# Attention, first group: who copies the last block's features, and how denominators are inverted

## The reference, cut to what matters

```python
H, d_head, scale = 16, 16, 6.0 ** -0.5
L_q = exterior(q1, q2)            # (B, T, H, 6), each of unit length
JL_k = exterior(k1, k2) @ J6.T
attn = einsum('bqhc,bkhc->bhqk', L_q, JL_k) * scale
attn = softmax(where(causal, attn, -inf), axis=-1)
v = (x @ W_v + b_v).reshape(B, T, H, d_head)
out = einsum('bhqk,bkhd->bqhd', attn, v).reshape(B, T, D)
return out @ W_o + b_o
```

## Time and profile before

| | us |
|---|---|
| median of 3 runs | 1147.47 |
| lowest, highest | 1146.25, 1149.84 |
| the profiled execution | 1146.05 |
| its span | 1144.3 |
| TensorE busy (matmuls) | 1036.2 |
| ScalarE busy | 874.3 |
| VectorE busy | 737.8 |
| GpSimd busy | 457.7 |

### The profile page before, as it was taken

The page is one execution under the profiler, slowest core; times in us unless marked ns, Lnnn a source line. Parts: engine busy times, 40 slices in busy tenths (PEclk is TensorE's granted clock), DMA queues, the critical chain, the costliest instruction groups (busy, mean ns, idle before and its releaser), DMA issues.

```text
span 1144.3 us, 23937 instructions
## 1 busy us (share of the span) xinstructions
PE 1036.2 (91%) x7549; PEld 564.4 (49%) x7549; DVE 737.8 (64%) x1471; ACT 874.3 (76%) x1251; POOL 457.7 (40%) x671
## 2 busy tenths in 40 slices
PE   8998999989888788998899898989899999999996
PEld 4457999946555121222122222222223578999844
DVE  6898788768997524434254657467758686445656
ACT  4226777746787999999999999999997237787710
POOL 1003666457730423422221322431312445677755
PEclk8999999999899899999999999999999999999999
DMA  8911555445776221020201122020100955566654
GB/s 288 276 57 49 172 164 170 154 129 168 211 220 193 66 71 51 11 66 10 65 11 31 40 70 80 26 78 19 48 1 19 300 171 157 162 189 184 185 163 153
DMA packets 125718, 133.82 MB, mean 117 GB/s; under 512 B 13224, under 2 KB 111888, under 8 KB 125616
## 3 DMA queue, kind: packets, MB, share of 16 engines
q1 hardware_dynamic: 109056, 90.95, 25.1%
q0 software_dynamic: 14448, 39.47, 12.4%
q10 hardware_dynamic: 2112, 2.10, 0.5%
HBM read 80.43 MB, written 52.04 MB: 116 GB/s over the span
## 4 chain that ended last, share of the span: by engine, by line
PE 30%; ACT 25%; issue 14%; DVE 8%; DVEq 1%; SPq 0%; POOL 0%; DMA 0%; ACTq 0%; POOLq 0%
ACT wide L2073 23%; PE banks L2445 6%; PE banks L1957 5%; PE banks L2370 4%; PE banks L2459 3%; PE banks L2379 2%; PE banks L1931 2%; PE banks L2433 1%; PE banks L1453 1%; PE banks L1456 1%; DVE x_res L1628 1%; DVE wide L1677 1%; PE banks L1971 1%; DVE attn_lines_parts L190 1%; PE banks L1455 1%
## 5 line engine op out<-in xcount | busy, mean ns | idle before, releaser
L2073 ACT ACTIVATE wide<-banks 128x1536 f32<-128x1536 f32 (+1 forms) x384 | 492.3, 1491 | 4.2 <-PE banks L1931 3.1
L1957 PE MATMUL banks<-wide,attn_attend_v_now 128*32 128x512 f32 (+3 forms) x2560 | 288.7, 542 | 2.4 <-POOL wide L2083 2.3
L2083 POOL TENSOR_SCALAR_AFFINE_SELECT wide<-wide 128x256 f32<-128x256 f32 (+1 forms) x320 | 115.9, 391 | 389.9 <-ACT wide L2073 387.4
L1931 PE MATMUL banks<-attn_attend_q_now,attn_attend_k_now 32*128 32x512 f16 (+3 forms) x1280 | 150.9, 355 | 56.8 <-ACT wide L2073 53.7
L1931 PEld LDWEIGHTS banks<-attn_attend_q_now,attn_attend_k_now 32*128 32x128 f16 x1280 | 38.7, 91 | 292.4 <-ACT wide L2073 248.5
L668 POOL DMA_INDIRECT f_region<-xn_rows,f_token_of x79 | 78.7, 996 | 125.1 <-DVE f_token_of L899 82.6
L2128 DVE COPY sums<-banks 128x512 f32<-128x512 f32 x32 | 22.1, 691 | 134.5 <-PE banks L1957 134.2
L2133 DVE RECIPROCAL below<-below 128x512 f32<-128x512 f32 x32 | 107.3, 3353 | 1.1
L2445 PE MATMUL banks<-f_xnt 128*128 128x128 f32 x752 | 100.3, 276 | 4.3 <-DVE f_more L2671 2.7
L2558 POOL DMA_INDIRECT last_rows_in<-xn_rows,f_spare x72 | 69.1, 960 | 64.0 <-DVE f_stage L2619 23.7
L2445 PEld LDWEIGHTS banks<-f_xnt 128*128 128x128 f32 x752 | 91.3, 191 | 6.6 <-issue 4.8
(11 more groups left out here) (368 smaller groups left out, 1783.3 us busy)
## 6 DMA issues: line engine op xcount, KB each, us to landing
y_half<-f_xnt SPq DMA_DIRECT2D x94, 128.0 KB
y_slots<-wide SPq DMA_DIRECT2D x79, 128.0 KB
attn_v<-f_more SPq DMA_DIRECT2D x32, 256.0 KB, 3.6
attn_attend_v_now<-attn_v SPq DMA_DIRECT2D x32, 256.0 KB, 3.2
x_res<-L_attn_x SPq DMA_DIRECT2D x8, 512.0 KB, 7.6
xn_rows<-f_w_all SPq DMA_DIRECT2D x8, 512.0 KB, 4.6
attn_q<-attn_lines_q_out SPq DMA_DIRECT2D x8, 512.0 KB, 3.4
attn_k<-attn_lines_k_out SPq DMA_DIRECT2D x8, 512.0 KB, 4.1
```

The costliest lines, as they stand in the source:

```text
L1931: last = pe.matmul(score[i % SLOTS][:, j, column:column + columns(u)], k_now[rows, kt * P:(kt + 1) * P], q_now[rows, qc * QW + c0:(qc + 1) ...
L1957: last = pe.matmul(out_bank[qc][rows, c0:QW], v_now[:, kt, rows], probs[:, place, column:column + columns(u)], start=(kt == 0), stop=(u == ...
L2073: act.activation(probs_flat[:, at:at + width_of[i]], score_flat[i % SLOTS][:, 0:width_of[i]], ACT.Exp, scale=SCALE).then_inc(sem.exp_done, 1)
L2083: pool.affine_select(out=part, in_=part, compare_op=ALU.is_ge, fill=0.0, base=0, pattern=[[0, part.shape[1]], [1, P]], channel_multiplier= ...
```

## The change

VectorE makes the second copies of the last block, right before its first chunk, and keeps the four turned parts behind its second chunk, one after the other; ScalarE does neither any more. TensorE's and SyncE's lists stay. The denominators are turned in 32x32 blocks, so that each block has them in one column; the 16 columns are inverted and turned back with each column repeated 32 times. The multiplication is the same.

```diff
-    def copy_last(act):
-        second_copies(act, BLOCKS - 1, (BLOCKS - 1) % 2)
-
-    def keep_last(act, part, held):
+    def copy_last(dve):
+        q = (BLOCKS - 1) % 2
+        dve.wait_ge(sem.parts_ready, BLOCKS)
+        both = feats[:, q, 0, :, 0:4 * PL].rearrange("p n (a c) -> p n a c", a=2)
+        dve.tensor_copy(both[:, :, :, PL:], both[:, :, :, 0:PL])
+        dve.tensor_copy(feats[:, q, 1, :, 2 * PL:4 * PL], feats[:, q, 1, :, 0:2 * PL]).then_inc(sem.feats_ready, 1)
+
+    def keep_last(dve, part, held):
         side, pair = part // 2, part % 2
-        act.wait_ge((sem.q_stored, sem.k_stored)[side], 16 * (BLOCKS - 1))
-        act.wait_ge((sem.q_turned, sem.k_turned)[side], 2 * (BLOCKS - 1) + pair + 1)
-        act.activation((q_out, k_out)[side][:, 2 * pair:2 * pair + 2, :].rearrange("p g n -> p (g n)"), held.bitcast(FP16), ACT.Copy
-                       ).then_inc((sem.q_ready, sem.k_ready)[side], 1)
+        dve.wait_ge((sem.q_stored, sem.k_stored)[side], 16 * (BLOCKS - 1))
+        dve.wait_ge((sem.q_turned, sem.k_turned)[side], 2 * (BLOCKS - 1) + pair + 1)
+        dve.tensor_copy((q_out, k_out)[side][:, 2 * pair:2 * pair + 2, :].rearrange("p g n -> p (g n)"), held.bitcast(FP16)
+                        ).then_inc((sem.q_ready, sem.k_ready)[side], 1)
...
+    shares = sb("shares", [P, QW // HR])
...
-    copied_at = (0, 4)
...
-                if (g, i) == copied_at:
-                    rest.copy_last(act)
-                if (g, i) in late_at:
-                    rest.keep_last(act, late_at[g, i], late_bank)
...
-            dve.sem_inc(sem.shuffle_turn, 1)
-            dve.stream_shuffle(below[:], sums[:], [(1 - side) * DH] * HR).then_inc(sem.chain_step, 1)
-            dve.wait_ge(sem.chain_step, 2 * (QC * g + qc) + 1)
-            dve.reciprocal(below[:], below[:]).then_inc(sem.chain_step, 1)
-            dve.wait_ge(sem.chain_step, 2 * (QC * g + qc) + 2)
+            dve.transpose(below[:], sums[:]).then_inc(sem.chain_step, 1)
+            dve.wait_ge(sem.chain_step, 3 * (QC * g + qc) + 1)
+            total = below[:].rearrange("p (b j) -> p b j", j=HR)[:, :, (1 - side) * DH]
+            dve.reciprocal(shares[:], total).then_inc(sem.chain_step, 1)
+            dve.wait_ge(sem.chain_step, 3 * (QC * g + qc) + 2)
+            dve.transpose(below[:].rearrange("p (b j) -> p b j", j=HR),
+                          shares[:].rearrange("p (b o) -> p b o", o=1).to_broadcast([P, QW // HR, HR])).then_inc(sem.chain_step, 1)
+            dve.wait_ge(sem.chain_step, 3 * (QC * g + qc) + 3)
...
             for qc in range(QC):
                 chunk(g, side, two, qc)
+                if (g, qc) == (0, 1):
+                    for part in late_at.values():
+                        rest.keep_last(dve, part, late_bank)
                 route_first(g, qc)
...
         dve.memset(second.minus_half, -0.5)
+        rest.copy_last(dve)
         groups(group)
```

More of the change, by code:

```diff
@@ L1761, in attend @@
     out_bank = [banks[:, 6 + qc % 2, :] for qc in range(QC)]
-    sem = semaphores(nc, tag, "w_loaded mask_turn stat_turn shuffle_turn load_turn scores_ready exp_done masked pv_done sums_kept chain_step holds_ready divided heads_ready "
+    sem = semaphores(nc, tag, "w_loaded mask_turn stat_turn load_turn scores_ready exp_done masked pv_done sums_kept chain_step holds_ready divided heads_ready "
                 "proj_done proj_added rest_kept stats_done")
```

## The result

| | before | after |
|---|---|---|
| median of 8 runs | 1147.37 | 1143.15 |
| lowest, highest | 1146.25, 1149.84 | 1139.9, 1147.05 |
| profiled execution (span) | 1146.05 (1144.3) | 1139.9 (1137.9) |
| mean granted TensorE clock | 0.981 | 0.988 |
| busy: TensorE, ScalarE | 1036.2, 874.3 | 1028.8, 870.4 |

The ratio is 0.9965, with a 95% interval of 0.9952 to 0.9978: faster by 4.2 us at the median, where the terms of the forecast made -4.9, and inside the range. (The time that was given, 1141.9, lies lower than the terms put it: it is the middle between a sum on the profiled execution and one on the median.) The profiled execution of after is the lowest of its eight runs, so its -6.15 us hold more than the change does. The two spans split at the first and the last exponential: 375.84 + 499.07 + 269.43 us before, 374.61 + 495.78 + 267.53 after.

A forecast was written before the change was run, and what follows sets the result against it. ScalarE was taken to bound the attention, with TensorE close behind. The terms 0 - 3.2 - 0.7 - 1.0 made -4.9 us; the forecast was 1141.9, the middle of 1141.15 and 1142.6, range from about 1139.4, somewhat below, to 1145.5.

The forecast's parts named there:

- The copies, 0: Two late-feature copies (lines 1492, 1493) off ScalarE: gain 0, since TensorE's unbroken work sets strip 10's start.
- The upper end of 1.47: Best case for moving the two copies off ScalarE before strip 10: a gain of 1.47 us.
- The loss of 0.5 by held cuts: Worst case for the copies: on VectorE they hold GpSimd's last mask cuts, and TensorE loses 0.5 us.
- The keeps, -3.2: Four keeps (line 1485) off ScalarE, strips 20 to 27: 3.6 us of gaps less 0.4 of TensorE slips, -3.2 us.
- The end of -2.0: Low end for the keeps' gain, if a stretch at TensorE's lower clock falls there: -2.0 us.
- The denominators, 2.4 us per chunk: VectorE's chain with transposes and short reciprocal shortens by 2.4 us per chunk, hidden for 31 of 32 chunks.
- Last masks, -0.7: Last six mask cuts: VectorE's long multiplication starts 0.7 us earlier, so -0.7 us; ends 0 and -1.1.
- Tail, -1.0: Behind the last chunk: TensorE's first two waits vanish and the third shrinks to 0.3, -1.0 us; ends 0 and -1.27.
- TensorE did not take the keeps back: Rival, chance 0.15: TensorE takes the keeps' time back, leaving 2.0 instead of 3.2; sum -2.5, 1144.3 us.
- Transposes were not dear: Rival, chance 0.04: dear VectorE transposes; at 3.35 us each no change, at 5 about 1151 us.
- The copies counted: Rival, chance 0.12: the copies bring their 1.47 us too and nothing slips; sum -7.4, 1139.4 us.
- Both VectorE gains fail: Rival, chance 0.07: last-mask and tail gains fail to arrive, only the keeps' -3.2 remains; 1143.6 us.

The follow-up runs named there:

- only_moves: Changed kernel with the old shuffle and reciprocal, so only copies and keeps move to VectorE: 1240.49 us, ratio 0.9981 to the kernel before.
- warmer: all_three plus matmuls nobody reads, before the first scores and behind strips 1 to 3: 1224.99 us, kernel before 1231.22. C is strip 10 to 26.
- marks_late: Changed kernel with VectorE's long multiplications (lines 1180, 1184) behind the last half add instead of in front of it: one execution of 1142.69 us.
- hint_late: Changed kernel with ScalarE's early load of the exponential's table moved behind its keeping of blocks HB and HB+1: one execution of 1142.04 us.
- changed_again: The changed kernel itself once more, on another chip: 1143.96 us in 12 runs, ratio 0.9975 to the kernel before.
- all_three_again: all_three repeated without further change: 1138.84 us in 6 runs, ratio 0.9921 to the kernel before.
- all_three: Changed kernel with hint_late's and marks_late's edits, and groups' last multiplication waiting for the next group's first ten mask cuts: 1139.75 us, ratio 0.9929.
- warm_copies_back: all_three plus 12 matmuls before the first scores and 8 behind strip 1's, nobody reading them, and the copies on ScalarE: one execution, 1141.21 us.
- copies_back: Changed kernel with the two copies on ScalarE again, behind strip 4: one execution of 1234.83 us.

## Why the prediction was right, and where not

*The copies, 0.* Right, and for the reason given: strip 10 hangs on TensorE's unbroken work at a partly lower clock. The exact statement is conditional, 0 to 0.2 as the clock rises here, and at least 0.74 where it is full. The upper end of 1.47 was not seen. The loss of 0.5 by held cuts did not come, though cuts were held: the copies took 0.37 and 0.57 us and held two cuts for 0.22 and 0.11 us. TensorE did not wait for them, and the kernels with the copies on VectorE lie on the same line as the one before.

*The keeps, -3.2.* -3.26 between strips 10 and 26. A keep took 0.69 us, the lower of the two ends. The walk through TensorE's slips held to 0.06 us. In `only_moves` it is -2.91: part of this gain needs the shorter chain. The end of -2.0, for a stretch at the lower clock in this place, was a real risk: `warmer` had one there, and its C of 21.75 leaves 1.88 of the gain.

*The denominators, 2.4 us per chunk.* From the copy's start to the multiplication's start it is now 397.46 - 394.95 = 2.51, where 740 + 3353 + 691 ns and gaps made 5.04; 2.5, with transposes of 0.71 instead of 0.74. For 31 chunks this was to be hidden. **This step failed in two of them**: I asked what waits for the chain, and not what its last two instructions would now lie beside. They met the first masks of the next group, and in groups 2 and 4 that cost time: +0.66.

*Last masks, -0.7.* **Failed**: -0.06 (TensorE waited 1.05 us instead of 1.11). The multiplication came 0.7 us earlier, as worked out: it started 0.68 behind the first of the six cuts before, and 0.01 ahead of it now. But the forecast passed these 0.7 us on to TensorE without a reason. The six cuts run one behind the other, and one of them is held for all of the multiplication wherever it lies among them: before it was the third, which began 0.06 behind the multiplication, and in after it is the first (2.00 us). The summary of the mask line over before's last six:

```profile
L2083 POOL TENSOR_SCALAR_AFFINE_SELECT wide<-wide x6: 287/416/1836, 869.2 to 872.8; 128x256 f32<-128x256 f32 x4, 128x128 f32<-128x128 f32 x2
```

The longest took 1.84 us before and takes 2.00 now, and the six take 3.89 against 3.95. The end of 0 was the truth. `marks_late` shows what there was to gain: 0.91.

*Tail, -1.0.* -0.71 to the third turning, by another way than forecast. The first wait vanished, but the time won there was lost again at the second turning, where 0.24 us of waiting for VectorE became 0.96 us for ScalarE, behind its table load: the second turning comes no earlier (11.77 and 11.78). The gain comes behind it: the third wait, 0.56 us, was forecast to shrink to 0.3 and vanished, and the turning starts 0.15 us closer to the product in front of it besides. That the sum came near is luck. I had followed one engine into the second turning and not the other; `hint_late` gives back 0.76.

*The sum.* By terms: 0 - 3.26 + 0.66 - 0.06 - 0.71 = -3.4, against a median difference of 4.2 here and 3.0 in `changed_again`. The -4.9 was 1.5 too much, in the three steps named: 0.66 in the groups, 0.64 at the last masks and 0.29 in the tail, less 0.06 that the keeps gave more. The terms fit both measured differences; that the first of them, 4.2, comes so near -4.9 is in part luck, as `changed_again` shows with 3.0 (1.6 to 4.1 by its interval). The profiled pair's -6.15 holds three things more. -1.23 lies before the attention, and -0.40 at strip 10, where the clock rose earlier in after. About -1.2 lies behind the third turning, in code that did not change: that rest takes 252.6 us in before, 251.4 in after, and 252.6 again in `changed_again`, so it is what executions of one kernel differ by, and its cause stays open.

*The rivals.* TensorE did not take the keeps back, though it is busier in the window (13.97 of 14.70 instead of 12.67). Transposes were not dear. The copies counted, but by tenths only. "Both VectorE gains fail" came closest of the rivals: the masks' gain failed, the tail's in part. Its 1143.6 is nearer to the measured 1143.15 than the forecast's 1141.9, and by the terms its -3.2 is nearer to -3.4 than the -4.9.

## What to carry to other kernels

When a chain gets shorter, look not only at who waits for it, but at what its instructions will now run beside: work of VectorE for which nobody waits can still hold GpSimd's instructions, and here GpSimd's cuts were on the path. When a wait is taken away, list every engine that the waiting instruction needs, since the releaser that the profile names is only the last one: here the other engine was 0.01 us behind it. And what leaves an engine in a stretch where TensorE runs at its lower clock is worth what TensorE lets through, which can differ from one execution to the next.

## What the runs showed of the hardware

- A mask cut on GpSimd (128x256 fp32) takes 0.40 to 0.41 us alone and up to 2.00 when it starts with a VectorE multiplication of two SBUF tensors that lasts 1.75; six beside a multiplication and an addition of 0.76 and 0.77 take 2.87 instead of 2.14. Beside VectorE's 16-bit copies within SBUF (0.37 and 0.57 us) two cuts take 0.62 and 0.52; beside a 32x32 transpose they stay at 0.41. VectorE pays too: the addition takes 0.77 under the cuts and 0.69 without. The Trainium skill's GPSIMD Engine Reference (Specifications) names this contention; the prices are these runs'.
- VectorE copies 1024 columns of fp16 from PSUM in 0.69 us, as long as 512 columns of fp32; ScalarE needed 1.12 to 1.26. The Trainium skill's VectorE: DVE Perf Modes (What auto-detection actually checks) has VectorE take a doubled mode where every tensor is 16-bit with step ±1, and these rows agree.
- A transpose in 32x32 blocks of 128x512 fp32 takes 0.711 us, a shuffle 0.740, a reciprocal of the same shape 3.353.
- Short stretches at the lower clock come at other places from one execution to the next. Group 0 took 62.47 us in `all_three_again` and 63.41 in `all_three`, the same kernel, whose window there reads:

```profile
433.70:437.40 3.70, 3.49 (x21) 0.60 (x25) 0.00 (x0) 3.06 (x4) 2.02 (x6) 0.54 0.00 0
```

ScalarE is busy for 3.06 of 3.70 us in it. The group is about 1 us longer by it, and the next one 0.33 shorter (60.99 instead of 61.32), in this kernel and in the three others that had a stretch at this place (`hint_late`, `marks_late`, `warm_copies_back`). A stretch inside group 5 (`hint_late`, `marks_late`) or group 6 (`copies_back`) goes with 1.5 us more. That is more than most terms of this study: a single execution's time can't judge those, the steps inside its trace can.
